# Attention, layer norm, LSTM and FP4 feed-forward in one kernel: x loaded from ScalarE, p's parts ahead of z, GpSimd's coarse product moved up

## The reference, cut to what matters

```python
# first half
x = x + attn2(attn1(x, cond))
# attn1: q, k, v = split(x @ c_attn_w + b), 16 heads of 16, one more key and value made of cond,
#   scores + causal mask + given mask, softmax over 65 keys, out @ c_proj_w + b
# attn2: q, k, v of attn1's result, relu(q), relu(k), kv = k^T v per head, out = q kv / (q . sum k),
#   layer_norm(out + attn1's result) * gamma + beta
# second half
x = x + ffn(lstm(x, h0=cond))
# lstm: 64 steps in time over all 64 sequences: a = x_t @ Wx + b + h @ Wh,
#   c = sigmoid(f) * c + sigmoid(i) * tanh(g); h = sigmoid(o) * tanh(c)
# ffn: fp4(t) rounds blocks of 16 to scale * {0, .5, 1, 1.5, 2, 3, 4, 6}, scale = max|block| / 6
#   h = silu(fp4(t) @ fp4(w_gate).T) * (fp4(t) @ fp4(w_up).T); out = fp4(h) @ fp4(w_down).T
```

## Time and profile before

| | |
|---|---|
| median of 3 runs | 917.55 us (912.46 to 919.34) |
| the profiled execution | 920.51 us, its span 918.8 us |
| PE busy | 753.5 us (82%) |
| DVE busy | 710.9 us (77%) |
| ACT busy | 466.2 us (51%) |
| POOL busy | 459.4 us (50%) |
| mean granted TensorE clock | 0.93 of full speed |

### The profile page before, as it was taken

How to read it: one execution, slowest core, us unless ns; L and a number is a source line. 1 busy time by engine, 2 the same in 40 slices (tenths; PEclk the granted TensorE clock), 3 DMA queues, 4 the chain that set the end, 5 groups by cost and what they waited for, 6 DMA issues and landing times.

```text
span 918.8 us, 23189 instructions
## 1 busy us (share of the span) xinstructions
PE 753.5 (82%) x7370; PEld 455.1 (50%) x7370; DVE 710.9 (77%) x1773; ACT 466.2 (51%) x1207; POOL 459.4 (50%) x596
## 2 busy tenths in 40 slices
PE   3336868788888888888767899999999999999965
PEld 2124545455555555555434455555555555555533
DVE  6077777777777777787553889999999999999983
ACT  2054656566777777777453444444444444444420
POOL 1045768877777777778630233333333333333342
PEclk9657878899999999999698999999999999999997
DMA  5865555677777777777501123332323333233333
GB/s 122 167 181 111 101 108 115 108 139 148 149 147 149 146 148 150 148 148 144 98 24 29 26 53 68 69 61 54 65 64 69 61 66 56 62 67 67 66 64 69
DMA packets 263438, 89.30 MB, mean 97 GB/s; under 512 B 233809, under 2 KB 262353, under 8 KB 263380
## 3 DMA queue, kind: packets, MB, share of 16 engines
q1 hardware_dynamic: 263380, 88.51, 48.5%
HBM read 25.45 MB, written 8.47 MB: 37 GB/s over the span
## 4 chain that ended last, share of the span: by engine, by line
DVE 27%; SPq 20%; issue 14%; PE 8%; ACT 4%; POOL 4%; DMA 3%; DVEq 1%; POOLq 0%; ACTq 0%
SPq L568 7%; SPq L541 5%; DVE fc L1511 4%; SPq L578 3%; PE bank L801 3%; DVE ffn_room L1577 3%; DVE prob L167 3%; DVE bank L164 3%; SPq L547 2%; DVE prob L171 2%; POOL xq L738 2%; DVE ffn_room L1569 2%; DVE ig L1513 1%; DVE bank L166 1%; DVE x_value L170 1%
## 5 line engine op out<-in xcount | busy, mean ns | idle before, releaser
L738 POOL TENSOR_TENSOR xq<-x_value,x_scale 128x256 f32<-128x256 f32 x32 | 29.4, 920 | 208.1 <-DVE x_value L171 208.1
L801 PE MATMUL bank<-gu,xqT 128*128 128x512 f16 (+1 forms) x576 | 127.3, 368 | 6.8 <-DMA xqT<-xq_split 6.8
L941 PE MATMUL bank<-wx,x1T 128*64 128x512 f16 x768 | 108.4, 406 | 8.1 <-DMA x1T<-x_split 7.5
L661 POOL TENSOR_TENSOR prob<-prob,row_max 128x520 f32<-128x520 f32 x64 | 73.7, 1152 | 74.7 <-DVE row_max L1393 74.2
L952 PE MATMUL bank<-wh,h 128*64 128x512 f16 x768 | 95.6, 385 | 0.7 <-ACT h L1215 0.7
L801 PEld LDWEIGHTS bank<-gu,xqT 128*128 128x128 f16 x576 | 56.0, 102 | 66.0 <-issue 13.2
L941 PEld LDWEIGHTS bank<-wx,x1T 128*64 128x64 f16 x768 | 73.8, 204 | 26.8 <-issue 8.2
L1030 PE MATMUL bank<-dn,hqT 128*128 128x256 f16 x576 | 70.3, 278 | 7.4 <-DMA hqT<-ffn_room 6.6
L668 POOL TENSOR_TENSOR p<-prob,p 128x512 f16<-128x512 f32 x64 | 71.6, 1119 | 2.2 <-ACT p L1112 2.2
L1030 PEld LDWEIGHTS bank<-dn,hqT 128*128 128x128 f16 x576 | 54.8, 99 | 26.3 <-issue 18.4
L759 POOL TENSOR_TENSOR ffn_room<-prob,h_fine 128x704 f16<-128x704 f32 x32 | 44.5, 1389 | 42.6 <-DVE h_rows L1522 42.6
(11 more groups left out here) (194 smaller groups left out, 1834.9 us busy)
## 6 DMA issues: line engine op xcount, KB each, us to landing
vimg_in<-image_values SPq DMA_DIRECT2D x64, 68.0 KB, 2.6
x_in<-in_x_columns SPq DMA_DIRECT2D x16, 256.0 KB, 3.0
x_res<-in_x SPq DMA_DIRECT2D x16, 256.0 KB, 3.1
x_rows<-x_rows_sb SPq DMA_DIRECT2D x32, 128.0 KB, 1.8
ffn_room<-x_rows SPq DMA_DIRECT2D x64, 64.0 KB, 2.2
out<-ffn_room SPq DMA_DIRECT2D x64, 64.0 KB, 2.0
add_mask<-in_mask_Bx1x1xS_ff SPq DMA_DIRECT2D x2, 512.0 KB, 7.5
qkT<-qk SPq DMA_TRANSPOSE x64, 4.2
```

What stands on the lines that cost most here:

```text
L661: pool.tensor_tensor(prob[:, r, :], prob[:, r, :], row_max[:, r, None].to_broadcast([P, 8, KEYS]), ALU.subtract).then_inc(s["shifted"], 1)
L738: pool.tensor_tensor(blocks(xq, D), blocks(fp4_x.value, D), spread(fp4_x.scale, D), ALU.mult).then_inc(s["xq_ready"], 1)
L801: last = pe.matmul(dst, lhs(a, c), rhs(b, c), start=first and c == 0 and a == b, stop=c == C - 1 and (a, b) == parts3[-1], skip_group_chec ...
L941: last = pe.matmul(bank[e][B * h:B * h + B, :], x1T16[m][:, c, :, at], half_cols(wx16, a, c, h), start=False, stop=True, skip_group_check= ...
```

## The change

Five things are changed, all in the order of instructions and in which engine issues two loads.

1. SyncE no longer loads x_in and x_res. ScalarE does, at the end of its step of the first stage: x_in for a pair in every other step as before, x_res now for one tile in every step, with a semaphore for each half of the buffer.
2. SyncE's step is now: qkT, p's first half, the extra values (vimg_in), p's second half, x1T, store of x1. Before: vimg_in, x_res or x_in, qkT, x1T, store of x1, both halves of p.
3. ScalarE's first stage: `probs_hi` of the first half stands right behind o_sum, then neg_mean and offset, then k2 and v2, `exp` and `probs_hi` of the second half, onT's high part, and only then z. GpSimd's product of z and gamma stands behind both low parts of p.
4. Second stage, GpSimd: the scale's two parts come first, then xq, and the coarse product no longer waits for xq_lo. VectorE: the product with up stands ahead of xq_lo.
5. Second stage, ScalarE: the gates of the tile's first time step stand ahead of the magnitude of the hidden rows.

```diff
@@ -211,3 +211,3 @@
-    x_pairs = x.rearrange("b s d -> (b s) d").rearrange("(n j p) d -> n p j d", j=2, p=P)
+    x_rows_tiles = x.rearrange("b s d -> (b s) d").rearrange("(n p) d -> n p d", p=P)
@@ -348,3 +348,3 @@
-    xres_loaded = sem("xres_loaded")
+    xres_loaded = [sem(f"xres_loaded{i}") for i in range(2)]
@@ -550,12 +550,3 @@  SyncE, first stage
         def step(tiles):
-            t1, t2, _, t4, _, t6 = tiles
-            if t1 and (t1.loop is not None or t1.b > 0):
-                image_values(t1)
-            if t4 and t4.parity == 0:
-                after(sp, s["xb_ready"], t4.count(back=1))
-                sp.dma_start(x_res[:, :, :], x_pairs[t4.pair()]).then_inc(xres_loaded, 16)
-            if t1 and t1.parity == 0 and (t1.loop is not None or t1.b < NT - 2):
-
-                sp.wait_ge(s["xT_lo"], t1.count(2))
-                sp.dma_start(x_in[:, :, :], x_cols_pairs[t1.pair() + 1]).then_inc(x_loaded, 16)
+            t1, t2, _, _, _, t6 = tiles
             if t1:
...
+            if t2:
+                probs_turn(t2, 0)
+            if t1 and (t1.loop is not None or t1.b > 0):
+                image_values(t1)
+            if t2:
+                probs_turn(t2, 1)
             if t6:
...
-            if t2:
-                probs_turn(t2, 0)
-                probs_turn(t2, 1)
@@ -698,7 +692,3 @@  GpSimd, first stage
-            if t5:
-
-                pool.wait_ge(s["z_ready"], t5.count())
-                pool.tensor_tensor(zg_rows[:, :], z_rows[:, :], gamma_sb[:, :], ALU.mult).then_inc(s["zg_ready"], 1)
             if t2:
                 probs_lo(t2, 0)
                 image_part(t2, 1)
                 probs_lo(t2, 1)
+            if t5:
+
+                pool.wait_ge(s["z_ready"], t5.count())
+                pool.tensor_tensor(zg_rows[:, :], z_rows[:, :], gamma_sb[:, :], ALU.mult).then_inc(s["zg_ready"], 1)
...
-                pool.wait_ge(xres_loaded, t4.pair_count())
+                pool.wait_ge(xres_loaded[t4.parity], t4.pair_count())
@@ -733,8 +727,2 @@  GpSimd, second stage
-            if t2:
-
-                pool.wait_ge(s["quant_x"], t2.count(Fp4.STEPS, Fp4.STEPS))
-                after(pool, s["xq_lo"], t2.count(back=1))
-                pool.tensor_tensor(blocks(xq, D), blocks(fp4_x.value, D), spread(fp4_x.scale, D),
-                                   ALU.mult).then_inc(s["xq_ready"], 1)
             if t4:
...
                 pool.tensor_tensor(h_fine[:, :], fp4_h.scale[:, :], h_coarse[:, :], ALU.subtract).then_inc(s["h_parts"], 1)
+            if t2:
+
+                pool.wait_ge(s["quant_x"], t2.count(Fp4.STEPS, Fp4.STEPS))
+                after(pool, s["xq_lo"], t2.count(back=1))
+                pool.tensor_tensor(blocks(xq, D), blocks(fp4_x.value, D), spread(fp4_x.scale, D),
+                                   ALU.mult).then_inc(s["xq_ready"], 1)
+            if t4:
                 pool.wait_ge(s["quant_h"], t4.count(Fp4.STEPS, Fp4.STEPS))
-                if t2:
-                    pool.wait_ge(s["xq_lo"], t2.count())
                 after(pool, hqT_in[0], t4.count(per=16, nth=16, back=1))
@@ -1146,2 +1139,10 @@  ScalarE, first stage
+            if t2:
+                probs_hi(t2, 0)
+            if t5:
+                act.wait_ge(s["mean_ready"], t5.count())
+                act.activation(neg_mean[:, :], mean_var[:, 0:1], ACT.Copy, scale=-1.0).then_inc(s["neg_ready"], 1)
+                act.wait_ge(s["neg_ready"], t5.count())
+                act.wait_ge(s["rstd_ready"], t5.count())
+                act.activation(offset[:, :], neg_mean[:, :], ACT.Copy, scale=rstd[:, 0:1]).then_inc(s["offset_ready"], 1)
             if t4:
...
+            if t2:
+                exp(t2, 1)
+                probs_hi(t2, 1)
+            if t3:
+                hi(t3, onT16[:, 0, :], bank[0][:, 0:D], "onT_ps", "onT_hi", "y_ps")
             if t5:
-                act.wait_ge(s["mean_ready"], t5.count())
-                act.activation(neg_mean[:, :], mean_var[:, 0:1], ACT.Copy, scale=-1.0).then_inc(s["neg_ready"], 1)
-                act.wait_ge(s["neg_ready"], t5.count())
-                act.wait_ge(s["rstd_ready"], t5.count())
-                act.activation(offset[:, :], neg_mean[:, :], ACT.Copy, scale=rstd[:, 0:1]).then_inc(s["offset_ready"], 1)
                 act.wait_ge(s["offset_ready"], t5.count())
...
-            if t2:
-                probs_hi(t2, 0)
-            if t3:
-                hi(t3, onT16[:, 0, :], bank[0][:, 0:D], "onT_ps", "onT_hi", "y_ps")
-            if t2:
-                exp(t2, 1)
             ffn_hi(t4, "outer")
-            if t2:
-                probs_hi(t2, 1)
@@ -1183,2 +1176,10 @@
                 act.activation(y_rows[:, t3.parity, :], bank[6][:, 0:D], ACT.Copy, scale=1.0 / W_P).then_inc(s["y_sb"], 1)
+            if t1 and t1.parity == 0 and (t1.loop is not None or t1.b < NT - 2):
+
+                act.wait_ge(s["xT_lo"], t1.count(2))
+                act.dma_start(x_in[:, :, :], x_cols_pairs[t1.pair() + 1]).then_inc(x_loaded, 16)
+            if t3:
+                after(act, s["xb_ready"], t3.count(back=2))
+                act.dma_start(x_res[:, t3.parity, :], x_rows_tiles[t3.number()]).then_inc(xres_loaded[t3.parity], 16)
+            if t3:
                 hi(t3, yT16[:, 0, :], bank[6][:, D:2 * D], "yT_ps", "yT_hi", "kv2_ps")
@@ -1227,2 +1228,4 @@  ScalarE, second stage
+            if t1:
+                lstm_gates(t1, 0)
             if t4:
...
                 fp4_h.magnitude(act, FF).then_inc(s["magnet_h"], 1)
             if t1:
-                lstm_gates(t1, 0)
                 lstm_tanh(t1, 0)
@@ -1570,6 +1572,2 @@  VectorE, second stage
-            if t2:
-                dve.wait_ge(s["xq_hi"], t2.count())
-                dve.tensor_tensor(xq_split[:, 1, :], xq[:, :], xq_split[:, 0, :], ALU.subtract).then_inc(s["xq_lo"], 1)
-            if t3:
                 dve.wait_ge(s["up_ps"], t3.count())
...
+            if t2:
+                dve.wait_ge(s["xq_hi"], t2.count())
+                dve.tensor_tensor(xq_split[:, 1, :], xq[:, :], xq_split[:, 0, :], ALU.subtract).then_inc(s["xq_lo"], 1)
```

## The result

| | before | changed |
|---|---|---|
| median | 917.44 us (912.46 to 919.34, 4 runs) | 972.4 us (965.71 to 976.18, 4 runs) |
| profiled execution, span | 920.51, 918.8 us | 965.71, 964.0 us |
| mean granted TensorE clock | 0.93 | 0.92 |

What follows compares the result with a forecast made beforehand. SyncE's queue was taken to bound attention, VectorE with TensorE nearly as full the second stretch. Attention 1.5 gained, first steps 2 lost, second stretch 9.9 gained, end 1 lost, about -9 with start steps: 908 us, range 893 to 920.

Steps and rivals of the forecast that it cites:

- Part 3: First stage, p ahead of z and p's transposes between qkT and x1T: zero, bounds -3 and +3 us.
- Rival D: Attention: loads leave SyncE but the pair stays 23.0 us as SyncE waits for p's parts; 908 to 910; 0.45 with forecast.
- Rival C: Attention: x_in's load lands late, at 5.5 us, making qk 3.1 us late; +22.5 us, 940; chance 0.12.
- Part 1: Attention, SyncE without its loads of x: 0.95 us a pair to be had, 9.5 us in 10 pairs.
- Part 2: ScalarE's later load of x_in: qk 0.8 us late a pair; attention nets 1.5 us gained, first steps 2 lost.
- Parts 4 and 5: Second stage, GpSimd's earlier coarse product and ScalarE's earlier gates: VectorE gains 0.9 us, 0.34 us a step, 9.9 us in all.
- TensorE's floor: Second stage: TensorE cannot go below 12.07 us a step; reaching it gives 0.51 us a step, 14.8 us.
- the long half: Second stage, first to second transpose of h on TensorE: 6.98 us stays, taken as 6.95.
- the short one: Second stage, second to third transpose of h on TensorE: VectorE needs 5.29 us, TensorE alone 5.19.

Runs made afterwards that it cites:

- e3: Kernel before, with only SyncE's transposes of p's two halves moved ahead of x1T and the store of x1: 967.44 us.
- e9: Changed kernel with x1T and the store of x1 back ahead of p's halves and the extra values back at the head of SyncE's step: 912.73 us.
- e5: Kernel before, with only the loads of x_in and x_res moved from SyncE to ScalarE, behind the copy of y_rows: 930.37 us.
- e8: e2 with both loads of x on ScalarE, x_in's early behind o_sum, x_res behind y_rows, SyncE's order else as before: 895.32 us.
- e2: Kernel before, with only the second stage's edits on GpSimd, VectorE and ScalarE: 903.54 us.
- e10: Changed kernel with only the load of x_in moved forward on ScalarE, behind the copy of o_sum: 952.06 us.
- e12: Kernel before, with only the second stage's edits on GpSimd and VectorE; ScalarE's gates stay behind the magnitude: 913.28 us.
- e6: Kernel before, with only the first stage's new order on ScalarE and GpSimd (p's high parts ahead of z, gamma product behind p's low parts): 914.77 us.
- e1: Changed kernel with x1T and the store of x1 put back ahead of p's two halves in SyncE's step: 929.14 us.
- e11: e7 with the extra values loaded behind both halves of p on SyncE, not between them: 885.13 us.
- e7: Changed kernel with two buffers for x1's halves and the load of x_in moved forward on ScalarE, behind the copy of o_sum: 889.71 us.

## Why the prediction was wrong

**The step that failed is Part 3**: "p's transposes on SyncE now sit between qkT and x1T ... a wait that SyncE's new slack of 1 us a step just covers. Zero, bounds -3 and +3 us." It measured +51.8 us in the kernel before (e3), and in the changed kernel SyncE's old order is worth 60.7 us (e9). The part asked whether SyncE can wait for p, and priced SyncE's time. It did not ask what stands behind p in the queue, who waits for that to land, and whether p itself hangs on it. x1T came 5 us later after qkT; the cover was about 0.8 us (x1T issued at 263.68, landing in 2.9 us by the median, the buffer written again at 267.34). And p's low part comes only after x1_hi has run, so each x1T waits for p and each p for the x1T ahead of it. Rival D had the place right, and priced it at nothing. Rival C had the sign, but its cause, the late load, is worth only 12.5 us (e5).

**Part 1** held: SyncE's relief is worth about 9.5 us where the load is in time (e8 against e2: 10.5; the step 11.03 us, forecast 11.04).

**Part 2** had one mechanism right, missed another, and its size was wrong. In e5 x_in lands 3.2 us after its issue, about as taken, and xT waits 1.3 us for it once a pair, instead of being 0.6 to 0.8 us late; a pair loses 2.1 us. Together with Part 1 it was netted to 0.5 us lost and measured 12.5 (e5), just beyond the outer ends of its two bounds together (5.5 and 6). It asked what the transposes do to the load, and had no term for what the load does to them: p's halves land 0.8 to 1.2 us later beside it (e5), and in the changed kernel x1T 1.0 us (e10).

**Parts 4 and 5** held. fc fell from 626 to 279 ns in the mean; the forecast was 9.9 us less 1 at the end, e2 measured 12.1, as TensorE's floor was reached (12.05 us a step) instead of 12.24. The working kept the long half at 6.95 us and gave the short one 5.29; they measured 6.87 and 5.17. By the Trainium skill (SBUF — State Buffer, section "Who interferes with whom") a GpSimd product that reads SBUF shuts out a VectorE instruction with two SBUF inputs; the trace agrees: every second fc took 0.97 us before, the others 0.29, and now all take 0.28. What this costs the kernel, though, depends on the half of the step: 5.0 us (e12) for 0.68 us in every second fc. By the same rule xq_lo was to wait 0.15 us, which does not show: it takes 0.42 us before and after.

**The sum.** The four parts each alone are -12.1 (e2), +12.5 (e5), -3.1 (e6), +51.8 (e3), together +49.1, and the whole is +55.0. The 6 us between them are within the noise: the interval of the whole alone is 6 us to each side. All but SyncE's order together, as e9 measured them, are -5.7, where e2, e5 and e6 add up to -2.7. In SyncE's order the extra values between p's halves count too: 19.2 us with x1T ahead of p (e9 against e1), 5.1 with two buffers and the early load (e11 against e7, not clear of noise). What they cost with x1T behind p and one buffer was not measured.

## What to carry to other kernels

When a DMA is moved in a queue, list all that then stands behind it, and for each the instruction that waits for its landing, buffer reuse included. On an in-order engine such a wait takes everything behind it along, and if what the moved DMA waits for is among it, the ring is closed and every step pays. A wait that does not show in the profile can still be near: take the moment at which the waiting instruction runs, subtract the DMA's start and its time to landing, and compare what is left with the shift (here 0.8 us with 5). A second buffer took away 59 us here with no instruction moved. And price a moved load also by the transfers that it will fly beside.

## What the runs showed of the hardware

With a 256 KB load from ScalarE's queue in flight, the transposing DMAs of SyncE's queue landed later in the same run: x1T in 3.6 us by the median instead of 2.6 (changed kernel), p's halves in 4.67 and 4.08 instead of 3.47 and 3.31 (e5). The load's own landing was 4.0 us in the changed kernel and 3.1 in e10. The Trainium skill (DMA: Bandwidth & Descriptors, section "Issuing engines are not separate DMA queues") says that a second issuer saves only issue time, and e5 agrees: x_in's landing was 3.0 us from SyncE and 3.2 from ScalarE. What the move to the second issuer changed is which transfers the load is in flight with.
